# Warm columns copied on chip, one loop for the keys, and early loads of x2 in a two-layer image kernel

## Chip, cores and metric

The kernel runs on one core of a Trainium2 chip. The metric is the device time in microseconds (us); lower is better. PE is the matmul engine, ACT, DVE and POOL are the scalar, vector and GpSimd engines, SP issues most DMAs.

## What is computed

The input x is [2, 64, 256, 256] in f32; the kernel sees it as 128 rows (batch times channel) of 65536 tokens. Four residual steps follow each other:

```python
x = x + shift_conv3x3(ln_c(x))                     # stage A; gives x1
t = t + recurrence(ln_t(t))                        # y_t = sigmoid(Wx_t + V y_{t-1}), Wx batch-normalized; gives x2
x = x + linear_attention(ln_c(x))                  # keys and values from every 4th row and column; gives x3
t = t + experts(ln_t(t))                           # top 8 tokens of each of 32 experts, two-layer FFN, scatter-add
# linear attention:
xs = x[:, :, 2::4, 2::4]                           # 4096 positions: the keys' stage
K = elu(k) + 1; V = v                              # kv = kv_w @ ln_c(xs) + kv_b
KV = sum_n K_n^T V_n (per head); Ksum = sum_n K_n
out = Q @ KV / (Q @ Ksum + eps); out = proj_w @ out + proj_b
```

## The kernel before

There are five stages, each a block of its own at whose end all engines meet.

**Stage A** (to 759 us) does the convolution and the projection W x and leaves x1 and the projected rows (`xl`) in DRAM.

**Region stage** (766 to 1081 us). The recurrence is cut into 8 regions of 8192 tokens, each region into 512 chunks of 16 tokens; one step advances all 512 chunks of a region at once. Since a chunk doesn't know the state at its start, it runs 12 warm steps over the last 12 inputs of the chunk in front (`WARM`), then its 16 own steps. A region lies in SBUF as `U[r % 4]`, [128, 16, 1 + 512]: column 0 holds the last chunk of the region in front, of which `load_warm` (L750) fetches the last 12 inputs from DRAM, in pieces of 4 bytes. A step is a product by V on PE (L814), an add of the input on DVE (L910) and a sigmoid on ACT (L836 and L827), for two groups of 256 chunks. Two regions are in work at a time: region r's 28 steps begin at slot 14 r. At step 15 of a region DVE keeps a state (L881) and compares the state reached by the warm steps with the true one (`check_states`, L890 and L894). POOL adds y to x1, one block of 2048 tokens in 5.5 us (L849), then picks the keys' positions out of it into `xsub` (L655). SP's list, per block k: store x2 of block k, load x1 of block k + 3, load a block of region r + 4; ahead of the first block of a region also `load_warm`. For the last region x1 is loaded over a free region buffer.

A **sequential fallback** (L935 to L1009) follows, which isn't taken in these runs.

**Keys' stage** (1081 to 1133 us). First a loop over 8 tiles of 512 keys (L1039, L1074, L1097): center on PE (L1043), square on ACT (L1079), mean of squares on PE (L1048), log and exp on ACT (L1084, L1088), scale on DVE (L1099). Then a loop over 16 pairs of 128-key groups (L1049, L1089, L1100): product with the key and value weights (L1056), bias on DVE (L1105), exp on ACT (L1093), max and min-add on DVE (L1111, L1113), and two matmuls for each group: the sum of K V (L1064) and the sum of K (L1066, one column of ones). At the end the masking by heads (L1117, L1118) and the product with the projection (L1069), copied at L1120.

**Attention stage** (1133 to about 1680 us): 32 blocks of x2 in a ring of 8 (`x2_ring`), loaded by `load` (L1234), four ahead of the first statistics. Squares (L1367 on ACT, L1439 on POOL), statistics (L1307, L1313), rstd to DRAM (L1240) and back as a broadcast (L1249), query (L1322, L1476), its map on ACT, POOL (L1444) and DVE, denominator, L1451 on POOL, attended (L1334), x3 (L1491), gates and top tokens. The **experts** close the kernel.

Of the kernel before, what the change touches and what calls it, by code (L numbers as in the profile page):

```python
# [7 lines left out]
F32 = mybir.dt.float32  # L8
I32 = mybir.dt.int32
U32 = mybir.dt.uint32  # L10
ALU = mybir.AluOpType
# [56 lines left out]
def build_program(nc, x, conv_k, ffn_w, ffn_v, gamma, beta, q_w, q_b, kv_w, kv_b, proj_w, proj_b,  # L68
# [4 lines left out]
    with stack:  # L73
# [568 lines left out]
        regions = ExitStack()  # L642
        stack.enter_context(regions)
        BUFS = 4
        U = [sb(f"region{j}", [P, CLEN, 1 + CHUNKS], F32, regions) for j in range(BUFS)]
# [4 lines left out]
        last_stored = sem("last_stored", keys)  # L650

# [8 lines left out]
        with ExitStack() as ph:  # L660
# [21 lines left out]
            dstep, dmm, zero_warm, last_x1_loaded = S("dstep"), S("dmm"), S("zero_warm"), S("last_x1_loaded")  # L682
# [50 lines left out]
            def wait_group(eng, r, j):  # L733

                b = r % BUFS
                warm_loads = r // BUFS + (1 if b else 0)
                eng.wait_ge(region_loaded[b][0], 16 * (GB * (r // BUFS + 1) + warm_loads))
                if j:
                    eng.wait_ge(region_loaded[b][j], 16 * GB * (r // BUFS + 1))
                elif r == 0:  # L740
                    eng.wait_ge(zero_warm, 1)

            @blk.sync
            def _(sp):
# [4 lines left out]

                def load_warm(r):  # L750
                    sp.dma_start(U[r % BUFS][:, CLEN - WARM:CLEN, 0:1],
                                 xl_d[r * RBLK - 1, :, :].rearrange("p (n c) -> p n c", n=CLEN)[:, CLEN - WARM:CLEN, BLOCK // CLEN - 1:BLOCK // CLEN],
                                 allow_slow_non_contiguous=True).then_inc(region_loaded[r % BUFS][0], 16)
# [20 lines left out]
                for k in range(LAST):  # L774
# [69 lines left out]
            def _(pool):  # L844
                pool.memset(U[0][:, :, 0:1], 0.0).then_inc(zero_warm, 1)
# [165 lines left out]

        with ExitStack() as ph:
            RING = 3
# [3 lines left out]
            t_kv = sb("t_kv", [P, RING, 2, 2 * P], F32, ph)  # L1017
            ek = sb("ek", [P, RING, 2, P], F32, ph)
            gm = sb("gm", [P, P], F32, ph)
            psa = [ph.enter_context(nc.psum_tensor(f"psa{j}", [P, TILE], F32)) for j in range(3)]  # L1020
            psb = ph.enter_context(nc.psum_tensor("psb", [P, TILE], F32))
            pkv = [ph.enter_context(nc.psum_tensor(f"pkv{j}", [P, 2, 2 * P], F32)) for j in range(2)]
            pg = ph.enter_context(nc.psum_tensor("pg", [P, P], F32))
            psum_k = ph.enter_context(nc.psum_tensor("psum_k", [P, 1], F32))
            pm = psb[:, 0:P]
            S = lambda n: sem(n, ph)
# [4 lines left out]
            NPAIR = NSUB // P // 2  # L1031

            @blk.sync
            def _(sp):
                sp.wait_ge(last_stored, 16 * RBLK)

            @blk.tensor
            def _(pe):
                for t in range(KT + 1):  # L1039
                    if t < KT:  # L1040
                        if t >= 3:
                            pe.wait_ge(kn, t - 2)
                        pe.matmul(psa[t % 3][:, :], center, xsub[:, t * TILE:(t + 1) * TILE], start=True, stop=True).then_inc(kc, 1)  # L1043
                    if t:
                        pe.wait_ge(ksq, t)
                        if t >= 2:
                            pe.wait_ge(kln, t - 1)
                        pe.matmul(psb[:, :], meanm, sqk[:, (t - 1) % 2, :], start=True, stop=True).then_inc(kv_, 1)  # L1048
                for c in range(NPAIR + RING - 1):  # L1049
                    if c < NPAIR:  # L1050
                        if c % (TILE // P // 2) == 0:
                            pe.wait_ge(kn, c // (TILE // P // 2) + 1)
                        if c >= 2:
                            pe.wait_ge(kvb_done, c - 1)
                        for i in range(2):
                            m = pe.matmul(pkv[c % 2][:, i, :], xsub[:, (2 * c + i) * P:(2 * c + i + 1) * P], kvT[:, :],  # L1056
                                          start=True, stop=True)
                        m.then_inc(kvp, 1)
                    d = c - (RING - 1)
                    if d >= 0:  # L1060
                        pe.wait_ge(kmap, d + 1)
                        for i in range(2):
                            first, last = d == 0 and i == 0, d == NPAIR - 1 and i == 1
                            pe.matmul(pg[:, :], t_kv[:, d % RING, i, P:2 * P], t_kv[:, d % RING, i, 0:P], start=first,  # L1064
                                      stop=last)
                            m = pe.matmul(psum_k[:, :], t_kv[:, d % RING, i, 0:P], ones[:, :], start=first, stop=last)  # L1066
                        m.then_inc(kvacc, 1)
# [821 lines left out]
```

## Time and profile before

| | us |
|---|---|
| median of 3 runs | 1936.65 (1932.2 to 1941.81) |
| profiled execution | 1939.52 |
| its span | 1937.7 |
| PE, DVE, ACT, POOL busy | 1562.9, 1440.2, 1237.0, 1451.2 |

Times in the profile count from the span's start. A row of the timeline gives start, length, engine, line of the code, operation, output and input tensors, and in square brackets the idle time in front of it and what ended it. "PEld" is the loading of weights, "SPq" the issuing of DMAs. An f32 matmul shows as two instructions.

### The profile page before, as it was taken

How to read it: one execution, taken by the hardware profiler on the slowest of the kernel's cores; microseconds unless marked ns; L12 is line 12 of the kernel's file. 1: busy time of each engine (PE TensorE's matmuls, PEld its weight loads, DVE VectorE, ACT ScalarE, POOL GpSimd, SP SyncE). 2: the span in 40 equal slices, each digit the busy share in tenths (PEclk: the TensorE clock that was granted, in tenths of full speed). 3: DMA queues.
4: the chain of work that ended last, by engine and by line, in shares of the span. 5: the costliest groups of instructions: out<-in, count | busy, mean ns of one | idle time of the engine just before them, and what ended most of it. 6: DMA issues, size and time to landing. Idle time of an engine off the chain costs nothing. (4 is left out here: it accounts for less than half of the span.)

```text
span 1937.7 us, 24495 instructions
## 1 busy us (share of the span) xinstructions
PE 1562.9 (81%) x5690; PEld 655.8 (34%) x5690; DVE 1440.2 (74%) x2310; ACT 1237.0 (64%) x2171; POOL 1451.2 (75%) x1070
## 2 busy tenths in 40 slices
PE   4899999999999983788786678999999999816100
PEld 1333333333333330356553343333333333205100
DVE  1689999999999984588887537999999999951000
ACT  2777777777777751588775448888888888620000
POOL 2999999999999990067777109999999999901670
PEclk8999999999999996799988779999999999955555
DMA  4578878888888655999996246888888888570111
GB/s 152 160 230 251 254 233 254 250 255 242 248 257 238 205 167 173 293 300 354 365 386 256 87 152 200 285 284 280 277 280 288 285 289 244 189 192 14 2 2 1
DMA packets 125343, 429.87 MB, mean 222 GB/s; under 512 B 57585, under 2 KB 62609, under 8 KB 80145
## 3 DMA queue, kind: packets, MB, share of 16 engines
q1 hardware_dynamic: 103520, 423.82, 69.2%
q10 hardware_dynamic: 18736, 4.29, 1.5%
q8 instruction: 50, 0.82, 0.2%
q0 software_dynamic: 2944, 0.18, 0.1%
q14 instruction: 93, 0.75, 0.1%
HBM read 257.93 MB, written 170.01 MB: 221 GB/s over the span
## 5 line engine op out<-in xcount | busy, mean ns | idle before, releaser
L454 ACT ACTIVATE tap_products<-xn,kk 128x512 f32<-128x512 f32 x384 | 275.2, 718 | 165.2 <-POOL x_and_products L485 159.8
L485 POOL TENSOR_TENSOR x_and_products<-tap_products,x_and_products 128x512 f32<-128x512 f32 x256 | 326.7, 1276 | 41.7 <-POOL x_and_products L485 3.5
L385 PE MATMUL pst<-xn,taps 128*128 128x512 f32 x768 | 351.8, 593 | 0.0
L1444 POOL TENSOR_SCALAR exp_q<-exp_q 128x512 f32<-128x512 f32 x128 | 189.3, 1479 | 81.9 <-ACT exp_q L1395 81.9
L910 DVE SCALAR_TENSOR_TENSOR pss<-region,bn,pss 128x256 f32<-128x256 f32 x432 | 196.5, 489 | 68.6 <-PE pss L814 66.4
L849 POOL TENSOR_TENSOR x_block<-x_block,region 128x2048 f32<-128x2048 f32 x28 | 155.2, 5542 | 116.2 <-ACT region L836 86.5
L543 DVE SCALAR_TENSOR_TENSOR pst<-xn,kk,pst 128x512 f32<-128x512 f32 x256 | 192.5, 752 | 61.7 <-PE pst L385 61.5
L385 PEld LDWEIGHTS pst<-xn,taps 128*128 128x128 f32 x768 | 145.5, 190 | 186.2 <-issue 186.0
L1439 POOL TENSOR_TENSOR sq_norm<-x_ring 128x512 f32<-128x512 f32 x128 | 188.4, 1472 | 5.7 <-DVE x_ring L1491 1.7
L485 POOL TENSOR_TENSOR x_and_products<-tap_products,x_ring 128x512 f32<-128x512 f32 x128 | 164.2, 1283 | 19.6 <-ACT tap_products L454 19.6
L425 ACT ACTIVATE sq<-x_ring 128x512 f32<-128x512 f32 x256 | 157.7, 622 | 16.1 <-POOL x_ring L492 10.1
L492 POOL TENSOR_TENSOR x_ring<-acc,x_and_products 128x512 f32<-128x512 f32 x128 | 163.4, 1277 | 0.6 <-DVE acc L543 0.6
L1451 POOL TENSOR_TENSOR q_z<-q_map,z_inv 128x512 f32<-128x512 f32 x128 | 163.7, 1279 | 0.0
L814 PE MATMUL pss<-region,vT 128*128 128x256 f32 x480 | 136.3, 410 | 19.5 <-ACT region L836 19.5
L568 DVE TENSOR_TENSOR wx<-psw,rstd_wide 128x512 f32<-128x512 f32 x128 | 137.7, 1076 | 17.7 <-DMA rstd_wide<-rstd_scratch 7.0
L1328 PE MATMUL ps_denominator<-q_map,dT 128*128 128x512 f32 x256 | 138.6, 623 | 9.7 <-DVE q_map L1485 8.4
L814 PE MATMUL pss<-warm_state,vT 128*128 128x256 f32 x352 | 109.7, 436 | 44.4 <-ACT warm_state L836 26.4
L1322 PE MATMUL ps_query<-x_ring,qcT 128*128 128x512 f32 x256 | 140.1, 631 | 5.0 <-DVE query L1476 5.0
L394 PE MATMUL psc<-x_ring,cst 128*128 128x512 f32 x256 | 139.6, 628 | 4.5 <-DVE xn L520 4.5
L400 PE MATMUL psw<-x_ring,wcT 128*128 128x512 f32 x256 | 132.9, 603 | 11.7 <-DVE wx L568 11.7
L836 ACT ACTIVATE region<-pss,bn 128x256 f32<-128x256 f32 x256 | 117.0, 474 | 29.5 <-DVE pss L910 28.4
L1401 ACT ACTIVATE ln_d<-ps_denominator,cols 128x512 f32<-128x512 f32 x128 | 86.8, 678 | 73.0 <-PE ps_denominator L1328 72.7
(243 smaller groups left out, 2981.0 us busy)
## 6 DMA issues: line engine op xcount, KB each, us to landing
rstd_wide<-rstd_scratch SPq DMA_DIRECT2D x128, 512.0 KB, 7.3
x_ring<-in_x SPq DMA_DIRECT2D x32, 1024.0 KB, 5.3
x_scratch<-x_ring SPq DMA_DIRECT2D x32, 1024.0 KB, 4.3
xl_scratch<-wx SPq DMA_DIRECT2D x32, 1024.0 KB, 8.7
region<-xl_scratch SPq DMA_DIRECT2D x32, 1024.0 KB, 11.4
x_ring<-x_scratch SPq DMA_DIRECT2D x32, 1024.0 KB, 5.2
rstd_of_channels<-rstd_scratch SPq DMA_DIRECT2D x64, 512.0 KB, 7.7
out<-x_ring SPq DMA_DIRECT2D x32, 1024.0 KB, 6.7
```

The source lines that it names most:

```text
L385: m = pe.matmul(wide(pst[g % 2]), taps[:, n * P:(n + 1) * P], tap_rows(g, t), start=(n == 0), stop=(n == len(PE_TAPS) - 1))
L425: act.activation(sq[l][:, g % TPB, :], x_tile(g), ACT.Square).then_inc(squared[l], 1)
L454: act.activation(prod[:, n, :, :], tap_rows(g, t), ACT.Copy, scale=kk[:, t:t + 1]).then_inc(products, 1)
L485: pool.tensor_tensor(xr[:, g % XR, :], prod[:, n, :, :].rearrange("p r w -> p (r w)"), xr[:, g % XR, :] if n else x_tile(g), ALU.add).then ...
L492: pool.tensor_tensor(x_tile(g), acc[:, g % 2, :, :].rearrange("p r w -> p (r w)"), xr[:, g % XR, :], ALU.add).then_inc(x1_ready, 1)
L543: dve.scalar_tensor_tensor(out=out, in0=tap_rows(g, t), scalar=kk[:, t:t + 1], in1=wide(pst[g % 2]), op0=ALU.mult, op1=ALU.add).then_inc(a ...
L814: pe.matmul(ps_at(r, j), vT[:, :], before, start=True, stop=True).then_inc(carried, 1)
L849: pool.tensor_tensor(in_chunks(x1_x2), in_chunks(x1_x2), y, ALU.add).then_inc(added, 1)
L910: dve.scalar_tensor_tensor(out=ps_at(r, j), in0=u, scalar=gain_w, in1=ps_at(r, j), op0=ALU.mult, op1=ALU.add).then_inc(summed, 1)
L1439: pool.tensor_tensor(sq[1][:, g % SQSLOTS[1], :], x_tile(g), x_tile(g), ALU.mult).then_inc(squared[1], 1)
L1444: pool.tensor_scalar(e, e, 1.0, None, ALU.min).then_inc(clipped, 1)
L1451: pool.tensor_tensor(qz[:, g % 2, :], qm[:, g % QSLOTS, :], zr[:, g % 2, :], ALU.mult).then_inc(qz_ready, 1)
```

## The change

Three parts. (1) The warm inputs of region r + 1 are no longer loaded: ACT copies them from the last column of region r, in front of region r's first sigmoid of the second group, before the states overwrite them. (2) The two loops of the keys' stage become one of 24 steps; the sum of K rides as a 129th column of the sum of K V, whose operands swap sides, so that a transpose and a copy are added at the end. (3) The ring of x2 is allocated in front of the keys' stage, and SP issues the loads of its first six blocks at the start of that stage. `xsub` lives on, and two buffers of the attention stage lie in it.

```diff
@@ region stage
             def wait_group(eng, r, j):
                 b = r % BUFS
-                warm_loads = r // BUFS + (1 if b else 0)
-                eng.wait_ge(region_loaded[b][0], 16 * (GB * (r // BUFS + 1) + warm_loads))
+                eng.wait_ge(region_loaded[b][0], 16 * GB * (r // BUFS + 1))
                 if j:
                     eng.wait_ge(region_loaded[b][j], 16 * GB * (r // BUFS + 1))
                 elif r == 0:
-                    eng.wait_ge(zero_warm, 1)
+                    eng.wait_ge(warm_ready, 1)
+                else:
+                    eng.wait_ge(warm_ready, r + 1)
...
-                    if r:
-                        load_warm(r)
...
                             sp.wait_ge(checked, r + 1)
-                            load_warm(r + BUFS)
...
+                def copy_warm(r):
+                    if r >= BUFS:
+                        act.wait_ge(checked, r - BUFS + 1)
+                    act.activation(U[r % BUFS][:, CLEN - WARM:CLEN, 0:1],
+                                   U[(r - 1) % BUFS][:, CLEN - WARM:CLEN, CHUNKS:CHUNKS + 1], ACT.Copy).then_inc(warm_ready, 1)
...
                             if s == 0:
                                 wait_group(act, r, j)
+                                if j == GROUPS - 1 and r + 1 < REGIONS:
+                                    copy_warm(r + 1)
@@ keys' stage
+        SLOTS, SEMS, AHEAD = 8, 3, 6
+        def load_x2(sp, k):
+            if k >= SEMS:
+                sp.wait_ge(x2_loaded[k % SEMS], 16 * (k // SEMS))
+            sp.dma_start(X[:, k % SLOTS, :], x2_d[k, :, :]).then_inc(x2_loaded[k % SEMS], 16)
...
-            RING = 3
+            RING = 4
+            V1 = P + 1
...
+            PAIRS = TILE // P // 2
+            SECOND, PRODUCT, SUM = 1, 6, 8
+            STEPS_K = NPAIR + SUM
...
             @blk.sync
             def _(sp):
+                for k in range(AHEAD):
+                    load_x2(sp, k)
                 sp.wait_ge(last_stored, 16 * RBLK)
...
+                def add_pair(p):
+                    pe.wait_ge(kmap, p + 1)
+                    pe.wait_ge(kst, 1)
+                    for i in range(2):
+                        m = pe.matmul(pg[:, :], t_kv[:, p % RING, i, 0:P], t_kv[:, p % RING, i, P:P + V1],
+                                      start=(p == 0 and i == 0), stop=(p == NPAIR - 1 and i == 1))
+                    m.then_inc(kvacc, 1)
+
+                for c in range(STEPS_K):
+                    if (t := tile_in(c, 0)) is not None:
+                        center_keys(t)
+                    if (p := pair_in(c, PRODUCT)) is not None:
+                        product(p)
+                    if (t := tile_in(c, SECOND)) is not None:
+                        second_moment(t)
+                    if (p := pair_in(c, SUM)) is not None:
+                        add_pair(p)
+                pe.wait_ge(kst, 2)
+                pe.transpose(pgt, gm[:, :], ident).then_inc(kmm, 1)
+                pe.wait_ge(kst, 4)
+                pe.matmul(pm, gv[:, :], pT[:, :], start=True, stop=True).then_inc(kmm, 1)
...
+                for c in range(STEPS_K):                       # ACT
+                    if (t := tile_in(c, 0)) is not None:
+                        square(t)
+                    if (t := tile_in(c, SECOND)) is not None:
+                        rsqrt(t)
+                    if (p := pair_in(c, PRODUCT)) is not None:
+                        exp_keys(p)
...
+                for c in range(STEPS_K):                       # DVE
+                    if (p := pair_in(c, PRODUCT)) is not None:
+                        add_bias(p)
+                    if (p := pair_in(c, PRODUCT + 1)) is not None:
+                        map_keys(p)
+                    if (t := tile_in(c, SECOND + 1)) is not None:
+                        norm(t)
...
@@ attention stage
-                    if (k := block_at(t, LOAD)) is not None:
+                    if (k := block_at(t, LOAD)) is not None and k >= AHEAD:
                         load(k)
```

`tile_in(c, lag)` is the tile whose work of that lag falls into step c (every second step), `pair_in` the pair.

## Rows read from the trace of the kernel before

**Rows 1.** Windows: stretch, length; busy of PE, PEld, DVE, ACT, POOL; clock, DMA, GB/s.
```profile
1081.00:1086.00 5.00, 4.35 (x6) 1.93 (x7) 0.00 (x0) 2.45 (x3) 0.00 (x0) 0.53 0.66 267
1103.00:1131.00 28.00, 26.56 (x182) 24.27 (x183) 20.87 (x48) 6.66 (x16) 0.00 (x0) 1.00 0.01 1
1200.00:1600.00 400.00, 400.00 (x1527) 130.01 (x1527) 376.46 (x564) 351.65 (x616) 396.69 (x287) 1.00 0.88 282
```

**Rows 2.** Timeline of the region stage, POOL's adds and DVE's comparison L890.
```profile
865.52 5.54 POOL L849 TENSOR_TENSOR x_block<-x_block,region 128x2048 f32<-128x2048 f32 x1 [5.96 <-ACT region L836]
869.84 1.77 DVE L890 TENSOR_TENSOR reached<-reached,region 128x512 f32<-128x512 f32 x1
...
895.77 5.54 POOL L849 TENSOR_TENSOR x_block<-x_block,region 128x2048 f32<-128x2048 f32 x1 [5.17 <-ACT region L836]
...
929.17 5.53 POOL L849 TENSOR_TENSOR x_block<-x_block,region 128x2048 f32<-128x2048 f32 x1 [2.98 <-ACT region L836]
930.35 4.91 DVE L890 TENSOR_TENSOR reached<-reached,region 128x512 f32<-128x512 f32 x1
...
963.82 5.53 POOL L849 TENSOR_TENSOR x_block<-x_block,region 128x2048 f32<-128x2048 f32 x1 [2.86 <-ACT warm_state L827]
964.56 5.33 DVE L890 TENSOR_TENSOR stats<-stats,region 128x512 f32<-128x512 f32 x1
...
996.69 5.53 POOL L849 TENSOR_TENSOR x_block<-x_block,region 128x2048 f32<-128x2048 f32 x1
998.93 3.83 DVE L890 TENSOR_TENSOR reached<-reached,region 128x512 f32<-128x512 f32 x1
```

**Rows 3.** Page, DMA issues of load_warm; windows without and with one such load.
```profile
region<-xl_scratch SPq DMA_DIRECT2D x7, 6.0 KB, 9.0
852.00:875.00 23.00, 19.28 (x82) 12.60 (x81) 20.71 (x44) 19.07 (x45) 16.85 (x7) 0.98 1.01 380
875.00:890.00 15.00, 15.00 (x63) 10.44 (x62) 13.72 (x31) 13.51 (x31) 14.13 (x5) 0.92 1.03 347
```

**Rows 4.** Groups by line, keys' stage: busy us, mean ns, idle before.
```profile
L1105 DVE TENSOR_TENSOR t_kv<-pkv,kvb 128x512 f32<-128x512 f32 x16 | 11.0, 691 | 5.6 <-PE pkv L1056 5.6
L1113 DVE SCALAR_TENSOR_TENSOR t_kv<-ek,t_kv 128x256 f32<-128x256 f32 x16 | 6.8, 425 | 0.6
L1093 ACT ACTIVATE ek<-t_kv 128x256 f32<-128x256 f32 x16 | 6.7, 416 | 20.3 <-DVE t_kv L1105 20.3
...
L1084 ACT ACTIVATE lnk<-psb,cols 128x512 f32<-128x512 f32 x8 | 5.5, 687 | 2.3 <-PE psb L1048 1.9
L1088 ACT ACTIVATE rsk<-lnk 128x512 f32<-128x512 f32 x8 | 5.0, 630 | 0.3
L1079 ACT ACTIVATE sqk<-psa 128x512 f32<-128x512 f32 x8 | 4.7, 590 | 1.9 <-PE psa L1043 1.9
L1111 DVE TENSOR_SCALAR t_kv<-t_kv 128x256 f32<-128x256 f32 x16 | 4.5, 284 | 0.0
```

**Rows 5.** Timeline of the keys' stage, PE and its weight loads.
```profile
1081.65 3.75 PE L1043 MATMUL psa<-xsub,cst 128*128 128x512 f32 x4 [16.00 <-PEq L935]
...
1086.30 1.02 PE L1043 MATMUL psa<-xsub,cst 128*128 128x512 f32 x2
...
1107.53 0.73 PEld L1056 LDWEIGHTS pkv<-kvT,xsub 128*128 128x128 f32 x4
...
1108.36 0.34 PEld L1064 LDWEIGHTS pg<-t_kv 128*128 128x128 f32 x2
```

**Rows 6.** Timeline, end of the keys' stage and start of the attention stage.
```profile
1131.42 0.29 DVE L1117 TENSOR_TENSOR gm<-pg,cst 128x128 f32<-128x128 f32 x1 [1.37 <-PE psum_k L1066]
...
1132.86 1.28 ACT L1360 ACT_TABLE_LOAD   x1 [3.69 <-PEq L1012]
...
1137.67 2.19 ACT L1367 ACTIVATE sq_norm<-x_ring 128x512 f32<-128x512 f32 x4 [3.52 <-DMA x_ring<-x_scratch]
...
1154.51 1.29 DVE L1476 TENSOR_TENSOR query<-ps_query,rstd_of_channels 128x512 f32<-128x512 f32 x2 [6.87 <-DMA rstd_of_channels<-rstd_scratch]
```

More of the change, by code:

```diff
@@ L641, in build_program @@
         gain_w = bn[:, 6:7]
[L642 to L645, printed above, removed]
         keys = ExitStack()
@@ L650, in build_program @@
         last_stored = sem("last_stored", keys)
+        regions = ExitStack()
+        stack.enter_context(regions)
+        BUFS = 4
+        U = [sb(f"region{j}", [P, CLEN, 1 + CHUNKS], F32, regions) for j in range(BUFS)]
         def take_keys(pool, block, src_rows):
@@ L1031, in build_program, with tile_in, pair_in @@
             NPAIR = NSUB // P // 2
+            PAIRS = TILE // P // 2
+            SECOND, PRODUCT, SUM = 1, 6, 8
+            STEPS_K = NPAIR + SUM
+            def tile_in(c, lag):
+                t, rest = divmod(c - lag, PAIRS)
+                return t if rest == 0 and 0 <= t < KT else None
+            def pair_in(c, lag):
+                p = c - lag
+                return p if 0 <= p < NPAIR else None
             @blk.sync
             def _(sp):
+                for k in range(AHEAD):
+                    load_x2(sp, k)
                 sp.wait_ge(last_stored, 16 * RBLK)
@@ L1049, in _ @@
[L1049 to L1067, printed above, removed]
@@ new lines, in product @@
+                def product(p):
+                    pe.wait_ge(kn, p // PAIRS + 1)
+                    if p >= 2:
+                        pe.wait_ge(kvb_done, p - 1)
+                    for i in range(2):
+                        m = pe.matmul(pkv[p % 2][:, i, :], xsub[:, (2 * p + i) * P:(2 * p + i + 1) * P], kvT[:, :],
+                                      start=True, stop=True)
+                    m.then_inc(kvp, 1)
+                def add_pair(p):
+                    pe.wait_ge(kmap, p + 1)
+                    pe.wait_ge(kst, 1)
+                    for i in range(2):
+                        m = pe.matmul(pg[:, :], t_kv[:, p % RING, i, 0:P], t_kv[:, p % RING, i, P:P + V1],
+                                      start=(p == 0 and i == 0), stop=(p == NPAIR - 1 and i == 1))
+                    m.then_inc(kvacc, 1)
@@ L1089, in _, with square @@
-                for c in range(NPAIR):
-                    act.wait_ge(kvb_done, c + 1)
-                    if c >= RING:
-                        act.wait_ge(kmap, c - RING + 1)
-                    act.activation(ek[:, c % RING, :, :], t_kv[:, c % RING, :, 0:P], ACT.Exp).then_inc(kexp, 1)
+                def square(t):
+                    act.wait_ge(kc, t + 1)
+                    if t >= 2:
+                        act.wait_ge(kv_, t - 1)
+                    act.activation(sqk[:, t % 2, :], psa[t % 3][:, :], ACT.Square).then_inc(ksq, 1)
@@ L1095, in _ @@
+                for c in range(STEPS_K):
[5 more added lines that the diff above has]
+                        exp_keys(p)
             @blk.vector
             def _(dve):
-                for t in range(KT):
+                dve.memset(t_kv[:, :, :, 2 * P:2 * P + 1], 1.0).then_inc(kst, 1)
@@ L1164, in build_program @@
             S = lambda n: sem(n, ph)
-            SEMS = 3
-            x2_loaded = [S(f"x2_loaded{r}") for r in range(SEMS)]
             x3_stored = [S(f"x3_stored{r}") for r in range(SEMS)]
```

121 lines of the change are left out of this document (56 added, 65 removed).

## Prediction

> **What bounds the kernel now.** I read the windows first, stage by stage, because a share over the whole span mixes five stages. The long last main loop (channel attention, from 1132.86 us) is bound by POOL: 396.69 us busy of 400 [rows 1]. Whatever lets that loop begin earlier moves the end by as much, and whatever makes one of its other engines faster moves nothing. The keys' stage before it (1081.65 to 1132.86 us, 51.2 us) has two halves one after the other: the norm, in which PE, ACT and DVE wait for each other, and the products, in which 16 pairs take 28 us [rows 1, 5], so 1.75 us a pair, with weight loads following each other without a gap. The region stage (766 to 1081 us) is a chain PE, DVE, ACT; the timeline of DVE and POOL shows one odd thing in it.
>
> **Region stage: where it stalls.** Once in a region DVE compares states at L890. Here it took 1.77 us where POOL's running add of 5.54 us had begun 4.3 us before it, but 4.91, 5.33 and 3.83 us where that add had just begun [rows 2]. Each time DVE ends about 0.5 us after POOL does: 929.17 + 5.53 = 934.70, against 930.35 + 4.91 = 935.26. So the stall is set by the lag between the moment POOL's block could begin and the moment it does. In the undisturbed regions the first block of a region follows the one before by 30.25 us (865.52, 895.77 [rows 2]), so that of region 3 could have begun at 926.0; it began at 929.17, a lag of 3.2 us. L890 begins 4.35 us after that release; by the same 4.35 the releases of regions 4 and 5 are 960.2 and 994.6, their lags 3.6 and 2.1, and the regions between last 34.2 and 34.4 us instead of 30.25: a us of lag costs 1.15 to 1.25. POOL was free there, and what it adds (x1) is loaded by a queue that is full: DMA share 1.01, 380 GB/s [rows 3]. The Trainium skill, page SBUF — State Buffer, section Who interferes with whom, says that GpSimd and a VectorE instruction with two SBUF inputs hold a shared port for a whole instruction and the other blocks; these rows agree.
>
> **Part 1, warm columns.** Seven DMAs of 6 KB go from SP's queue [rows 3]; each has 1536 pieces of 4 bytes (128 partitions x 12 steps). Price of one: the stretch of 15 us with one of them moves 347 GB/s against 380 without [rows 3], so 15 x (1 - 347/380) = 1.3 us of a full queue; the two other such stretches that I looked at gave the like, and I take 1.25. The first three lie in the initial loads, before anything waits for them, and count as nothing. The later ones are issued ahead of the x1 loads of regions 3 and 4: three before block 12 (3.75 us), four before blocks 16 to 20 (5.0 us). Block 12 could then start at 929.17 - 3.75 = 925.4, but is released at 926.0: lag 0, gain 34.2 - 30.25 = 4.0. Block 16 then is released at 956.25 and starts at 963.82 - 5.0 = 958.8: lag 2.5 instead of 3.6, gain 1.2. Block 20: 996.69 - 5.0 = 991.7 against a release at 956.25 + 30.25 + 2.9 = 989.4: lag 2.3 instead of 2.1, loss 0.3. Sum 4.9, less the copies on ACT: seven instructions that the trace doesn't show. The nearest row is an ACT instruction of 256 columns, 0.416 us [rows 4]; 12 columns cost no more, so at most 2.9 us for all, at least nothing. What is queued behind a copy on ACT is the first sigmoid of the second group, and five of the seven come just ahead of a comparison whose end POOL fixes, so they vanish in it. The other two I take at 0.2 each. The waits that the copy adds are on states checked two regions ago and on loads that the next instruction wants anyway. **Region stage: -4.5**, bounds -10 (all lags gone: 4.0 + 4.1 + 2.4 less the copies) and +4 (the copies in full, and blocks landing so that one comparison more meets an add that has just begun).
>
> On small pieces the Trainium skill has a rule against this price: DMA: Bandwidth & Descriptors, section Why small descriptors are slow, gives some 3 cycles of overhead a packet. By that a warm load would be an estimated 96 x 4 cycles an engine, as much as 1.5 pieces of 8 KB, 0.5 us instead of 1.25, and the region stage would give some 2 us. The two windows decide for 1.25.
>
> **Part 2, the keys' loop.** Per tile of 512 columns there are one centering, one second moment and two pairs. PE: a pair's product is four instructions of 256 columns, with weight loads from 1107.53 to 1108.36 [rows 5], 0.83 us, 0.21 each. With 512 columns the two instructions of a centering or a second moment hold PE for twice that each, 0.85 us together (they show as 1.02 with the latency at their end). A pair's sums have the rest of 1.75, 0.92, for eight instructions. The change has four of these (the column of ones rides as the 129th), so 0.46. Per tile 2 x 0.85 + 2 x (0.83 + 0.46) = 4.3 us. DVE per tile: 0.69 (the norm, as long as the bias add) + 2 x (0.691 + 0.284 + 0.425) = 3.49; ACT: 0.590 + 0.687 + 0.630 + 2 x 0.416 = 2.74 [rows 4]. So PE is the bound where the loop is full, and the lag of the steps leaves each product at least 2.1 us of other PE work before its sum, against 1.7 us that a bias, a map and their hops need.
> Start: six steps carry no product. ACT does the square, then waits for the second moment, then log and exp, then the next square: 0.59 + 1.02 + 0.69 + 0.63 and hops = 3.0 us a tile, the first 4.1 (PE at its low clock in 1081 to 1086, granted 0.53 [rows 1]). With the first product allowed after the third second moment: 1081.65 + 4.1 + 3.0 + 3.0 = 1091.7.
> Full part: five tiles at 4.3 less the two sums not yet due, 5 x 4.3 - 0.92 = 20.6: to 1112.3.
> Drain: six pairs without norm, where the round product, bias, map, sum binds: DVE's 1.40 with gaps, 1.5 each, 9.0: to 1121.3, and the last pair's bias, the map before it, its own map and its sum (0.69 + 0.71 + 0.71 + 0.46 and hops) 2.8: 1124.1, where the old stage has its masking at 1131.42 [rows 6].
> Tail: the old one takes 1.44 us from there to the next stage (1132.86); the transpose and its copy add one more trip PE and DVE, 0.35 + 0.49 + 0.29 = 1.1. Next stage at 1126.6. **Keys: -6.3.** Bounds: if every tile of the full part costs PE and DVE waits as the old norm did (some 20% more, 4 us) -2; if start and drain overlap better, -9. Six x2 loads run meanwhile; DMA is idle in that stretch (0.01 [rows 1] in 1103 to 1131), so 6 MB at 380 GB/s, 17 us, fit into 45. SP holds nothing else then. Their cost is taken as nothing; if they weren't hidden, part 3 would be smaller.
>
> **Part 3, start of the attention.** Now ACT's first square waits for the first x2 block: 1137.67, where the table load begins at 1132.86 and takes 1.28 [rows 6], so it could be at 1134.1: -3.5. PE's sums of x then come early too, and the chain square, second moment, variance, rstd, DRAM, broadcast, first query at 1154.51 [rows 6] moves with it. PE comes out of a busy loop instead of 5 us of waiting, and the broadcast of 1 MB has no x2 load right behind it. Between 0 and 2 us more for both; I take 0.5. **-4.0**, bounds -3.5 and -5.5. Behind it POOL runs without a gap, so the shift reaches the end. The buffers that moved into xsub and the earlier ring change no order: nothing.
>
> **Sum.** -4.5 - 6.3 - 4.0 = -14.8. The profiled execution, 1939.52 us, of which 1937.7 are the span, would be 1924.7. It lies 2.9 above the median of the three runs, 1936.65; that median would be 1921.9.
>
> **Rivals.** (a) *The region stage gives nothing and the loop runs worse than its PE sum.* POOL's blocks reach the comparisons by chance, and a shift by 1 to 5 us can turn a lag of 0 (as in regions 1 and 2) into one of 3. For it: three of eight comparisons now vary by up to 3.6 us. Against: the blocks of regions 1 and 2 in the rows are released by ACT, not by a load. Region 0, keys -4, attention -3.5: -7.5, 1929.2. (b) *Slower: PE's clock.* In 1081 to 1086 the granted clock was 0.53, the low level (1.2 GHz), after 16 us without work, and 1.00 (2.4 GHz) in 1103 to 1131 [rows 1]. In the new start PE has 1.7 us of work in 3.0. Were the low level kept through the loop, a tile would be 8.6 us: 12 + 5 x 8.6 - 1.8 + 6 x 2.6 + 6 = 75 us instead of 51, +24, and with the two other terms +15.5: 1952. It outweighs all gain from 3.4 tiles at the low level (14.8 / 4.3). Against: the norm part of before, where PE also waits for ACT, went at the high level (two instructions of 512 columns in 1.02 us at 1086.30 [rows 5]). The Trainium skill, TensorE: Matmul & The Clock Gate, section What's actually happening, says that the low level is the default and activity releases it; on a loop with PE as its bound it speaks for the full level. (c) *The x2 loads are hidden anyway or don't run early.* If they waited for the stage's end part 3 would be 0: -10.8, 1925.9. SP's list has them first, so little speaks for it.
>
> **Chances.** Forecast with its own spread 0.64, (a) 0.22, (c) 0.06, (b) 0.05, the rest (a cause that no row shows) 0.03. About 0.5%, 9.7 us, is what a measurement of this kernel can tell from no change (its three runs spread by as much). Of the forecast and (c), some 0.68 end beyond it; (a) is within it, as is what is left of the forecast: 0.26; slower 0.06. The range takes (a) in with some noise, above, and the bounds of the region stage and the keys together, below: 1911 to 1932.
>
> **What would show it.** L890 at 1.8 us also in region 3, the second stretch of DMA at 375 GB/s or more; the warm copy at some 0.2 us on ACT. Keys' stage 45 us, PE idle only in its first 10 and last 12 us, clock 1.00 from its first 5 us on. Attention: no wait for x2, first query 17 to 18 us after the stage begins (21.65 now); POOL without gaps from then. Wrong if L890 stays at 4 to 5 us, if a step of the loop shows PE waiting for the map, or if the clock falls in the loop.

## Result, and the profile after

| | before | after |
|---|---|---|
| median, 15 runs each | 1936.65 us (1931.28 to 1941.81) | 1925.02 us (1920.68 to 1929.09) |
| ratio, 95% interval | 1 | 0.9945 (0.9933 to 0.9956) |
| profiled execution, its span | 1939.52, 1937.7 | 1924.74, 1922.9 |
| PE, DVE, ACT, POOL busy | 1562.9, 1440.2, 1237.0, 1451.2 | 1556.5, 1435.2, 1238.3, 1450.8 |

The change saves 11.6 us; 14.8 had been forecast. The busy time of POOL is the same within 0.4 us; what moved is when the long loop begins. (Two of the six runs of experiment 7 fell into a slower state, at a lower granted clock, and are left out of its time.) So the trace is best read as a ledger of stages: each stage's length from the first row of one to the first row of the next. The columns are the region stage (first DMA issued to the first centering of the keys), the keys' stage, the attention stage up to its first query, and from there to POOL's last work in it.

| us | region | keys | to first query | then |
|---|---|---|---|---|
| before | 315.2 | 51.2 | 21.65 | 543.3 |
| before, profiled again | 315.1 | 51.3 | 21.67 | 543.3 |
| after | 309.8 | 45.8 | 18.1 | 543.6 |
| after, profiled again | 310.6 | 49.4 | 18.3 | 543.3 |
| after, a third time | 311.2 | 47.4 | 17.7 | 542.9 |
| mean difference | **-4.6** | **-3.7** | **-3.6** | 0.0 |
| forecast | -4.5 | -6.3 | -4.0 | 0 |

The three sum to -11.9, and the medians differ by 11.6. The two first profiles alone differ by 14.8, the forecast to the tenth, but by luck: in the one of after stage A came out 2.3 us shorter and the experts 1.5 us longer, and the keys' stage was the shortest of three.

Three profiles are few. The kernel of experiment 3 has the region stage of after as it is, that of experiment 7 too; theirs took 312.2 and 307.4 us. Over the five profiles the stage takes 307.4 to 312.2 us, 310.2 in the mean, which is 4.9 under before. The keys' stage of after stands unchanged in the kernels of experiments 3, 8, 9 and 10, where it took 46.3, 46.0, 47.4 and 46.3 us; over seven profiles the mean is 46.9, 4.3 under before.

**Region stage.** The timeline of after answers [rows 2]: L893 is the comparison, L852 POOL's add, L820 the new copy on ACT.

```profile
924.00 5.54 POOL L852 TENSOR_TENSOR x_block<-x_block,region 128x2048 f32<-128x2048 f32 x1 [2.59 <-ACT region L839]
928.32 1.77 DVE L893 TENSOR_TENSOR reached<-reached,region 128x512 f32<-128x512 f32 x1
...
957.70 5.54 POOL L852 TENSOR_TENSOR x_block<-x_block,region 128x2048 f32<-128x2048 f32 x1 [2.34 <-DMA x_block<-x_scratch]
957.71 0.21 ACT L820 ACTIVATE region<-region 128x12 f32<-128x12 f32 x1
958.57 5.22 DVE L893 TENSOR_TENSOR stats<-stats,region 128x512 f32<-128x512 f32 x1
...
993.09 3.22 DVE L893 TENSOR_TENSOR reached<-reached,region 128x512 f32<-128x512 f32 x1
```

The add of block 12 is released by ACT, 4.3 us ahead of the comparison, which takes 1.77 us where it took 4.91. (In [rows 2] the profile puts that add down to ACT as well; in the second profile of before it waits 2.85 us for its load.) Block 16 still waits for its load, and the comparison beside it still takes 5.22 us. The windows show the queue (columns as in [rows 1]; the first is a stretch of [rows 3], the second the stretch of another warm load, in which before moved 343 GB/s, the third lies in the long loop).

```profile
875.00:890.00 15.00, 15.00 (x68) 10.21 (x67) 14.84 (x34) 14.39 (x34) 12.53 (x6) 0.99 1.02 377
911.00:926.00 15.00, 14.40 (x64) 9.24 (x62) 14.19 (x32) 14.16 (x32) 10.17 (x5) 1.00 1.01 368
1180.00:1600.00 420.00, 419.17 (x1597) 136.15 (x1596) 394.78 (x592) 369.72 (x647) 416.61 (x301) 1.00 0.88 283
```

The first stretch moves 377 GB/s, where a warm load had left 347 [rows 3]. In the last line POOL is busy for 416.61 of 420 us, and PE for 419.17. The prediction named POOL as the bound of this loop; PE's row is as full, here and in [rows 1], and no run tells the two apart. What the account needs, that the loop passes on whatever comes earlier, is shown by the last column of the ledger, which doesn't change.

**Keys' stage.** PE's rows at the start of the new loop, centering (L1076), second moment (L1082) and first product (L1089):

```profile
1074.05 2.05 PE L1076 MATMUL psa<-xsub,cst 128*128 128x512 f32 x2 [16.00 <-PEq L938]
1076.78 2.08 PE L1082 MATMUL psb<-sqk,cst 128*128 128x512 f32 x2 [0.69 <-ACT sqk L1123]
...
1081.06 1.12 PE L1082 MATMUL psb<-sqk,cst 128*128 128x512 f32 x2 [0.69 <-ACT sqk L1123]
...
1084.11 1.12 PE L1082 MATMUL psb<-sqk,cst 128*128 128x512 f32 x2 [1.07 <-ACT sqk L1123]
...
1085.93 1.89 PE L1089 MATMUL pkv<-kvT,xsub 128*128 128x256 f32 x8
...
1117.65 0.29 DVE L1182 TENSOR_TENSOR gm<-pg,cst 128x128 f32<-128x128 f32 x1 [0.81 <-PE pg L1097]
```

A second moment is two instructions of 512 columns: 2.08 us for the pair of them shows the low clock (1.2 GHz), 1.12 the high one (2.4 GHz). Tiles are 4.28 us apart, then 3.05. From the first product to the masking (L1182) it is 31.7 us.

**Attention stage.** The rows that answer to [rows 6]:

```profile
1119.82 1.28 ACT L1411 ACT_TABLE_LOAD   x1 [3.84 <-PEq L1031]
1121.11 2.71 ACT L1418 ACTIVATE sq_norm<-x_ring 128x512 f32<-128x512 f32 x5
...
1137.96 1.29 DVE L1527 TENSOR_TENSOR query<-ps_query,rstd_of_channels 128x512 f32<-128x512 f32 x2 [6.02 <-DMA rstd_of_channels<-rstd_scratch]
```

The square starts when the table is loaded, with no wait for x2 in front (3.52 us before). The first query comes 18.14 us into the stage, against 21.65.

### The profile page after: what moved, and what is told of

It reads as the page before. It is cut to its first block and busy times, and to the rows that moved or that the text cites. A ratio compares the mean times of both kernels' runs of the same rounds, so it can differ in the third digit from the quotient of the medians.

```text
span 1922.9 us, 24399 instructions
## 1 busy us (share of the span) xinstructions
PE 1556.5 (81%) x5627; PEld 648.4 (34%) x5627; DVE 1435.2 (75%) x2312; ACT 1238.3 (64%) x2178; POOL 1450.8 (75%) x1070
## 5 line engine op out<-in xcount | busy, mean ns | idle before, releaser
L852 POOL TENSOR_TENSOR x_block<-x_block,region 128x2048 f32<-128x2048 f32 x28 | 155.3, 5545 | 110.8 <-ACT region L839 88.5
L425 ACT ACTIVATE sq<-x_ring 128x512 f32<-128x512 f32 x256 | 157.6, 622 | 16.7 <-POOL x_ring L492 10.1
L807 PE MATMUL pss<-region,vT 128*128 128x256 f32 x480 | 137.5, 411 | 18.4 <-ACT region L839 18.2
L400 PE MATMUL psw<-x_ring,wcT 128*128 128x512 f32 x256 | 132.9, 603 | 11.6 <-DVE wx L568 11.6
L839 ACT ACTIVATE region<-pss,bn 128x256 f32<-128x256 f32 x256 | 116.6, 474 | 29.4 <-DVE pss L913 28.7
```

The source lines that it names most:

```text
L425: act.activation(sq[l][:, g % TPB, :], x_tile(g), ACT.Square).then_inc(squared[l], 1)
L807: pe.matmul(ps_at(r, j), vT[:, :], before, start=True, stop=True).then_inc(carried, 1)
L852: pool.tensor_tensor(in_chunks(x1_x2), in_chunks(x1_x2), y, ALU.add).then_inc(added, 1)
```

## Experiments: which part gives what

**1. Warm copies alone.** The kernel before, with part 1 of the change only: `copy_warm` on ACT in place of `load_warm`.

```diff
-                    if r:
-                        load_warm(r)
...
                             if s == 0:
                                 wait_group(act, r, j)
+                                if j == GROUPS - 1 and r + 1 < REGIONS:
+                                    copy_warm(r + 1)
```

> The kernel before with part 1 alone (warm columns copied by ACT). Theory (three terms that add up; the warm loads' share of a full DMA queue sets the lag of POOL's adds): the region stage, from its first DMA issue to the first centering of the keys, goes from 315.2 us to 309 to 311, L890 in region 3 at 1.8 us instead of 4.9; the total falls by 4 to 6 us. Rival (chance alignment of POOL's adds and DVE's comparisons, the warm loads not the cause): the stage lies anywhere between 309 and 318, total within 2 us of before.

Measured: 1934.25 us, ratio 0.9987 (0.997 to 1.0003) to before in the same session, as in all that follow; region stage 310.9 us, -4.3, the other stages within 0.1 us.

```profile
911.00:926.00 15.00, 14.39 (x65) 9.34 (x64) 14.82 (x34) 14.92 (x35) 10.76 (x4) 1.00 1.01 375
...
926.56 5.54 POOL L854 TENSOR_TENSOR x_block<-x_block,region 128x2048 f32<-128x2048 f32 x1 [2.25 <-DMA x_block<-x_scratch]
929.38 3.27 DVE L895 TENSOR_TENSOR reached<-reached,region 128x512 f32<-128x512 f32 x1
```

The stretch moves 375 GB/s where before moved 343, so a warm load costs 15 x (1 - 343/375) = 1.3 us of a full queue; the other stretch gives 1.2. The stage gains what the forecast had for it, though not by the same comparison each time: block 12 is held by its load here, and the comparison takes 3.27 us, where 1.8 had been expected. In the three profiles of after that comparison took 1.77, 4.58 and 3.16. The gain doesn't sit in one lag. One profile couldn't exclude the rival, chance alignment; that all six profiles whose kernel has the copies and no other edit in this stage have it at 307.4 to 312.2 us, against 315.1 twice, does speak for the copies. For the total 4 to 6 us had been expected; it gains 2.5 by the ratio, and the interval takes in no change: the runs bear out the 4.3 us in the stage, not in the time.

**2. Each warm load twice.** The kernel before, with an addition: a second load of the same 6 KB into spare memory.

```diff
 def load_warm(r):
+    sp.dma_start(spare[:, r - 1, :, 0:1], xl_d[...]).then_inc(spare_loaded, 16)
     sp.dma_start(U[r % BUFS][:, CLEN - WARM:CLEN, 0:1], xl_d[...]).then_inc(region_loaded[r % BUFS][0], 16)
```

> The kernel before with each warm load issued twice (the second into a spare tile that nothing reads, on a semaphore that is waited for at the end of the stage). Theory: the price doubles: each extra load takes 1.25 us of the full DMA queue, blocks 12 and 16 start 3 to 5 us later, region stage 317 to 321 us, total 2 to 6 us over before; the DMA rate in a stretch of 15 us around two such loads falls to 310 to 325 GB/s. Rival (packet overhead of some 0.5 us a load): at most 2 us in all, rate 335 or more.

Measured: 1939.08 us, ratio 1.0011 (0.9998 to 1.0024); region stage 317.5, +2.4. The stage is where it was expected; the total isn't clear of no change, and 2 to 6 us had been expected.

```profile
932.64 0.68 DVE L896 TENSOR_TENSOR reached<-reached,region 128x512 f32<-128x512 f32 x1
934.09 5.55 POOL L855 TENSOR_TENSOR x_block<-x_block,region 128x2048 f32<-128x2048 f32 x1 [4.63 <-DMA x_block<-x_scratch]
...
875.00:890.00 15.00, 15.00 (x65) 10.40 (x64) 14.11 (x32) 13.62 (x32) 12.18 (x5) 0.94 0.95 276
...
ACT warm_state L833 <- DMA region<-xl_scratch: 5.6, 1, 5.6
```

The queue falls to 276 GB/s in this stretch and to 296 in 911 to 926, further than the 310 to 325 expected of a doubled price. POOL's add (block 8 here) waits 4.63 us for its load. The comparison now ends before the add begins, and takes 0.68 us: that is its own duration with POOL idle. So the stall isn't in the comparison's work. A later POOL even frees it: the next two comparisons take 0.68 us as well. That would explain why twice the loads cost the stage only 2.4 us, though ACT now waits once for a region's load (5.6 us, last line; its columns are total, count, longest). The step of the forecast "a us of lag costs 1.15 to 1.25" holds only up to the point where the add starts behind the comparison.

**3. The early loads of x2 away.** The kernel after, with the six loads at their old place.

```diff
-        SLOTS, SEMS, AHEAD = 8, 3, 6
+        SLOTS, SEMS, AHEAD = 8, 3, 0
```

> The changed kernel without the early loads (parts 1 and 2 only; all x2 loads in the attention stage as before). Theory: keys' stage 45.5 to 46 us as in the changed kernel, first query 21.5 us after the attention stage begins instead of 18.1, total 3.5 us over the changed kernel. Rival (the early loads cost the keys' loop or are hidden anyway): keys' stage shorter than 45.5 and the total within 1 us of the changed kernel.

Measured: 1929.95 us, ratio 0.9966 (0.9953 to 0.9979), 3.2 us over after in that session (1926.79, below); keys' stage 46.3, to the first query 21.3.

```profile
1124.52 1.28 ACT L1411 ACT_TABLE_LOAD   x1 [4.15 <-PEq L1031]
...
1129.30 2.19 ACT L1418 ACTIVATE sq_norm<-x_ring 128x512 f32<-128x512 f32 x4 [3.50 <-DMA x_ring<-x_scratch]
```

The wait for x2 is back, 3.50 us, and with it 3.2 us of the stage. Part 3 is worth that, and the loads cost the keys' stage nothing that can be seen: 46.3 without them, 45.8 to 49.4 with them, and from the first product to the masking 31.7 us either way. Rival (c) falls.

**4, 5, 6. The same kernels again.** The keys' stage in the first profile of after was 45.8 us; is that its length?

> The changed kernel itself. Theory: stages as in its first profile, region 309, keys 45.8, start of the attention 18.1 us, total 10 to 15 us under before. Rival (its first profile was a lucky one): a region stage of 312 us or more.

> The kernel before, once more, for its stages. Theory: region stage 315 +- 1 us, keys 51.2, first query 21.6 us after the stage begins; what differs between executions is the clock in the first microseconds of a stage and the experts' part. Rival: the region stage varies by 3 us or more with how POOL's adds fall against DVE's comparisons, so that the gain read there from one pair of profiles says little.

> The changed kernel, a third profile. Theory: region 309 to 311 us; keys' stage 45.8 or, if PE's clock rises late, up to 49.4. Rival: it rises as early as in the first profile nearly always, keys 45.8 to 46.3.

Measured: after 1926.79 us, ratio 0.9941 (0.9919 to 0.9963), and 1929.23 in a single run; before 1941.14 in a single run. Before repeats its stages to 0.1 us; after's keys' stage is 49.4 and 47.4, where the first had 45.8, so the first profile was a lucky one in this stage. PE in the former, and the windows over it:

```profile
1079.65 2.07 PE L1082 MATMUL psb<-sqk,cst 128*128 128x512 f32 x2 [0.69 <-ACT sqk L1123]
...
1084.12 2.07 PE L1082 MATMUL psb<-sqk,cst 128*128 128x512 f32 x2 [0.69 <-ACT sqk L1123]
...
1088.58 2.07 PE L1082 MATMUL psb<-sqk,cst 128*128 128x512 f32 x2 [0.69 <-ACT sqk L1123]
...
1092.16 2.17 PE L1089 MATMUL pkv<-kvT,xsub 128*128 128x256 f32 x8
...
1082.00:1086.00 4.00, 3.31 (x5) 0.85 (x4) 0.69 (x1) 1.68 (x3) 0.00 (x0) 0.50 1.01 424
1086.00:1090.00 4.00, 3.31 (x5) 1.16 (x4) 0.69 (x1) 1.91 (x3) 0.00 (x0) 0.50 1.01 418
1094.00:1098.00 4.00, 4.00 (x18) 2.84 (x17) 3.04 (x8) 2.86 (x6) 0.00 (x0) 1.00 0.35 145
```

The granted clock is 0.50, the low level (1.2 GHz), until 1092.7, 15.8 us after the loop began, with PE busy for 3.31 us of 4; in the first profile it rises 6.0 us in, and the pair at 1081.06 was fast. A tile then takes 4.46 us instead of 3.05, and the first product comes 15.2 us after the first centering instead of 11.9 (third profile: the clock rises 11.3 us in, the product comes at 13.5). From the first product to the masking all three take 31.7 to 32.0. So nearly the whole spread of the stage lies in its start, and goes with the clock there.

## Experiments: what can still be had

**7. Two edits at the starts.** The kernel after, with the second moment of a tile two steps later, so that two centerings stand ahead of the first wait and ACT isn't waited for in each tile; and without the loading of the ACT table at the start of the attention stage (the keys' stage has left the same table in place).

```diff
-            SECOND, PRODUCT, SUM = 1, 6, 8
+            SECOND, PRODUCT, SUM = 3, 6, 8
...
-                act.preload_act_table_set("natural_log_exp_and_others")
```

> The changed kernel with the second moment two steps later in the keys' loop (so that the next tile's centering and square run ahead of it) and without the table load at the head of the attention stage, whose table is the one of the keys' stage. Theory: start of the loop 2.1 us a tile instead of 3.05, keys' stage 2 to 3 us shorter, and less hanging on when PE's clock rises; attention's first square 1.3 us earlier, first query 16.9 us after the stage's begin instead of 18.2; total -3 to -4. Rival (PE's total work bounds the stage, the start is hidden in it): keys' stage unchanged at 45.8.

Measured: 1920.4 us (four runs), ratio 0.9911 (0.9883 to 0.9939) to before; keys' stage 42.4, to the first query 16.7.

```profile
1076.31 1.20 PE L1082 MATMUL psb<-sqk,cst 128*128 128x512 f32 x2
...
1078.38 1.10 PE L1082 MATMUL psb<-sqk,cst 128*128 128x512 f32 x2
...
1080.63 1.89 PE L1089 MATMUL pkv<-kvT,xsub 128*128 128x256 f32 x8
...
1115.20 2.71 ACT L1417 ACTIVATE sq_norm<-x_ring 128x512 f32<-128x512 f32 x5 [3.97 <-PEq L1031]
```

Tiles of the start are 2.07 us apart, PE has no gap of 0.69 us for the square, and the first second moment, 3.6 us after the first centering, already goes nearly at the high clock. The first product comes 7.9 us after the start. From there to the masking it is 32.3 us, 0.3 to 0.6 more than in after: only the start was gained. The square of the attention stage begins with the stage, 1.3 us earlier. Not all of the total is the edit's: the region stage is that of after, but came out at 307.4 us, 3.1 under the mean of three. The stages, not the total, say what the edits are worth: 4.5 to 5.1 us in the keys' stage, by the mean it is held against, and 1.3 in the next.

**8. The last region's adds all on DVE.** After the last comparison DVE and POOL add two blocks each. The kernel after, so changed that DVE adds all four.

```diff
-            POOL_LAST = (1, 3)
+            POOL_LAST = ()
```

> The changed kernel with all four last adds of y on DVE instead of two on POOL. Theory (DVE's and POOL's adds take turns at the shared input, so the end is their sum: 5.7 us each on POOL, some 3.7 each on DVE): from the last sigmoid to the end of the last add 15 to 16 us instead of 18.9, total -3. Rival (they run side by side and DVE's 12 us are its own two adds of 6): 24 us, total +5.

Measured: 1921.53 us, ratio 0.9912 (0.9889 to 0.9935). First two lines of after, then two of this kernel.

```profile
1051.31 5.39 DVE L893 TENSOR_TENSOR reached<-reached,region 128x512 f32<-128x512 f32 x1 [0.54 <-ACT region L839]
1057.54 11.99 DVE L925 TENSOR_TENSOR region<-region 128x2048 f32<-128x2048 f32 x2
```

```profile
1053.76 0.69 DVE L893 TENSOR_TENSOR reached<-reached,region 128x512 f32<-128x512 f32 x1 [0.54 <-ACT region L839]
1055.29 15.08 DVE L925 TENSOR_TENSOR region<-region 128x2048 f32<-128x2048 f32 x4
```

With POOL idle the four adds take DVE 15.08 us, 3.8 each. Of the two in after the first took 8.24 us, begun beside POOL's second add and ended 3.7 after it, and the second 3.83. So DVE didn't work more slowly beside POOL; it waited for it, in the comparison and in its first add. The adds take DVE's time after POOL's, and two engines finish this work later than one: from the comparison's start to the end of the adds it is 18.2 us with both, 16.6 with DVE alone. That is 1.6 gained, where 3 had been expected. The median is 3.5 under that of after; what is above the 1.6 isn't explained by the edit.

**9. The comparison's subtraction on POOL.** The kernel after; POOL subtracts ahead of the region's first add, DVE only reduces, and SP waits for the subtraction.

```diff
+                def subtract_states(r):
+                    pool.wait_ge(y_ready, y_done(r))
...
+                    pool.tensor_tensor(d, d, U[r % BUFS][:, CLEN - 1, 0:CHUNKS], ALU.subtract).then_inc(subtracted, 1)
...
                         if s == HALF + 1 and r:
                             keep_state(r)
+                        if s == HALF + 3 and r:
                             check_states(r - 1)
```

> The changed kernel with the subtraction of the state comparison on POOL, ahead of the region's first add, and DVE's reduction two steps later; SP waits for the subtraction where it waited for the comparison. Theory (the stall is DVE waiting for POOL's running add through its second SBUF input, and is paid on the chain): no stall of 2.7 us and more at the comparison, regions follow each other in 27.5 to 28 us instead of 30.2 to 34, region stage 290 to 298 us instead of 309, unless the DMA queue (8.4 us a block, 33.6 us a region) takes over, in which case it is 298 to 305 with waits for the region's load. Rival (the stall is DVE's own, from reading one column of a strided tile): POOL's subtraction is as long and something else is late; region stage 306 us or more.

Measured: 1925.57 us, ratio 0.994 (0.992 to 0.996); region stage 304.6, 5.9 less than the mean of after. The profiled execution took 1922.22 us. The ratio is that of after (0.9945), so the gain shows in the stage of one profile and not in the time.

```profile
951.26 5.53 POOL L853 TENSOR_TENSOR x_block<-x_block,region 128x2048 f32<-128x2048 f32 x1 [2.29 <-ACT warm_state L840]
957.22 1.26 POOL L862 TENSOR_TENSOR stats<-stats,region 128x512 f32<-128x512 f32 x1
958.51 0.69 DVE L903 TENSOR_REDUCE dmax<-stats 128x1 f32<-128x512 f32 x1 [5.13 <-POOL stats L862]
```

The stall is now an idle time in front of DVE's reduction, 5.13 us: POOL's add of an older block stands ahead of the subtraction. Part of the wait only changed its name. The subtraction itself takes POOL 1.26 us, and ACT waits once for a region's load (6.6 us): of what had been expected, the case in which the DMA queue takes over (298 to 305 us) is the one that fits.

**10. The reduction later.** Kernel 9 with the reduction six slots later.

```diff
-                        if s == HALF + 3 and r:
+                        if s == HALF + 9 and r:
```

> As sub_pool, but DVE's reduction eight steps after the old comparison instead of two. Theory (in sub_pool DVE waited for POOL's subtraction, which stood behind POOL's adds in their queue, so the wait had only changed its name): with the reduction late enough no wait of more than 1 us is left at it, the regions follow each other in 27.5 to 28.5 us until the DMA queue holds POOL's blocks, region stage 295 to 301 us (sub_pool 304.6, the changed kernel 309.8). Rival (the chain is held by the DMA queue already): 303 to 305 as in sub_pool.

Measured: 1920.39 us, ratio 0.992 (0.9901 to 0.9939); region stage 304.9, the same as in 9. The theory had 295 to 301; the rival, 303 to 305, came true.

```profile
916.84 0.59 ACT L831 ACTIVATE warm_state<-region,bn 128x256 f32<-128x256 f32 x1
943.72 0.59 ACT L831 ACTIVATE warm_state<-region,bn 128x256 f32<-128x256 f32 x1
...
979.59 0.60 ACT L831 ACTIVATE warm_state<-region,bn 128x256 f32<-128x256 f32 x1 [7.33 <-DMA region<-xl_scratch]
...
1047.42 0.69 DVE L903 TENSOR_REDUCE dmax<-reached 128x1 f32<-128x512 f32 x1 [16.60 <-POOL reached L862]
```

While nothing stalls, regions are 26.9 us apart (916.84 to 943.72) instead of 30.25. But then ACT waits 7.33 us for a region's load, and at the end DVE waits 16.60 for POOL, which itself had waited 25.6 us in all for x1. Each comparison's stall is gone, and waits for loads have taken its place. That the queue now bounds the stage is how I read these rows; no run took traffic off it to test that.

**11, 12. Together.** Kernel 11 is 7, 8 and 9 in one; kernel 12 is 7, 8 and 10.

> The changed kernel with the three edits of sub_pool, last_dve and starts together. Theory: their gains are in stages one after the other and add up: 12 to 20 us under the changed kernel, 1905 to 1913. Rival (the region stage is held by the DMA queue once the stalls are gone): 6 to 9 us under it.

> The changed kernel with sub_pool_late, last_dve and starts together. Theory: stages add up: region 292 to 298 us, keys 42.5 to 43, first query after 16.7; total 1905 to 1911. Rival (what the region stage gains is lost to the last adds or to x1 loads that come later): 1913 to 1916 as all_four.

Measured: 1914.96 us, ratio 0.9881 (0.9861 to 0.9902), and 1914.99, ratio 0.9885 (0.9864 to 0.9907). Stages of 11: region 303.0, keys 42.9, to the first query 16.7; of 12: 302.7, 42.2, 16.5. Both are some 10 us (0.5%) faster than after and 22 to 24 faster than before in their sessions. The later reduction adds nothing to 11, as experiment 10 had it. Stage by stage the parts do add up: 310.5 - 5.9 (experiment 9) - 1.6 (experiment 8) is the 303.0 of the region stage. Neither kernel came to the 1913 and 1911 us at the upper end of what was expected, because the region stage had been expected at less than experiments 9 and 10 gave. For kernel 12 the rival theory, 1913 to 1916, is the one that held.

## Why the prediction was right, and where it was off

**Time, range and direction** held: 1925.0 for 1921.9, inside 1911 to 1932. The miss of 3.1 us is nearly all in one term.

**Region stage, -4.5 forecast, -4.3 alone and -4.6 in the mean.** The price of a warm load (1.25 us) was measured as 1.2 to 1.3. (By their packets alone it is less: 96 on each of 16 engines, 9.1 ns each in the trace of before, 0.87 us.) By the rule of the Trainium skill, page DMA: Bandwidth & Descriptors, section Why small descriptors are slow, the estimate had been 0.5 us; the trace doesn't agree. In detail the sum was less good than its total. Comparisons of regions 3 and 4 are now 928.32 and 958.57, 30.25 us apart, where they were 34.2: the 4.0 of the forecast, but in this profile only. In the second that interval is 33.75 us, in the third 31.7. The next interval is 34.5 (34.4 before): the 1.2 that was to be gained there isn't. The one after is 31.6 (33.45 before, from 998.93 to L890's next at 1032.38): 1.8 that I hadn't counted. So that the total of this term came out at -4.3 to -4.6 is in part luck. The copies on ACT cost 0.21 us each, inside the bound.

One thing in it the prediction had no term for. It took 30.25 us as the undisturbed distance of two regions. The second profile of after has shorter ones; the windows go from comparison to comparison (columns as in [rows 1]).

```profile
840.10:868.76 28.66, 25.03 (x109) 16.42 (x109) 26.53 (x59) 24.86 (x58) 24.07 (x9) 1.00 0.94 337
868.76:897.44 28.68, 25.04 (x109) 16.45 (x110) 26.54 (x60) 24.83 (x58) 24.16 (x9) 1.00 1.01 377
897.44:927.73 30.29, 26.66 (x109) 17.91 (x109) 26.71 (x59) 25.00 (x58) 21.36 (x9) 0.94 1.01 365
```

The comparison takes 1.8 us in all three. Where PE's mean granted clock is 1.00 a region takes 28.7 us, where it is 0.94 it takes 30.3, and in before it is 0.94 in each of the regions that the prediction calls undisturbed. PE waits for ACT around each comparison (2.41 us in front of 843.36 in before) and then runs its next products at the low level. So 1.6 us of a region's length goes with the clock after the stall, and with it about half of what the regions gain in experiment 10 (clock 1.00, 26.9 us).

**Keys' stage, -6.3 forecast, -3.7 measured: the term that was mis-sized.** The working had the first product 10.05 us after the start (4.1 + 3.0 + 3.0), then 32.4 us to the masking and 2.5 to the next stage. Measured: 11.9, 15.2 and 13.5 (mean 13.5), 31.7 to 32.0, and 2.2. The PE sum of the full part and the drain was right within 0.7 us; the start was 3.5 us too short. Two things were missing from its sum. First, the code puts the fourth tile's centering in front of the first product; that is 0.86 us at the high level (1085.07 to 1085.93) and 1.71 at the low one (1090.45 to 1092.16 in the second profile). Second, the low clock was taken to end with the first tile ("4.1", then 3.0 and 3.0), from the rows of the old loop [rows 5], where four instructions of centering stood in a row (3.75 us) and the next were fast 4.6 us after the start. The new loop begins with two, then waits 0.69 us for ACT in each tile, and stayed at 0.50 for 6.0 to 15.8 us: its first three tiles took 4.6, 3.4 and 3.05 us in the first profile, 4.6, 4.5 and 4.5 in the second. Rival (b) named this mechanism. Its 12 us for a start at the low level were near what the second profile has for these three tiles (13.5); what it had wrong is that the low level would last through the full part of the loop, which it did in no profile. In the start a tile at the low level cost 1.4 us more (4.46 - 3.05).

Experiment 7 shows the other side: with two centerings in a row at the start the clock rose after 3.9 us, and in the two kernels of experiments 11 and 12, which begin in the same way, after 5.1 and 3.0. In the four profiles of the old loop it rose after 3.9 to 5.4 us, in seven of the new one, started as in after, after 6.0 to 15.8. That goes with how a loop starts; why the same kernel needs 6 us once and 15.8 another time stays open. The Trainium skill, page TensorE: Matmul & The Clock Gate, section What's actually happening, has activity release the low level; the trace agrees.

**Attention, -4.0 forecast, -3.6 measured.** The sure part, the wait for x2 of 3.5 us, was right (3.2 in experiment 3). The extra 0.5 wasn't there: from the issue of the broadcast to the first query it took 7.4 us in both kernels (1130.54 to 1137.96 here), and the first second moment of the stage went at the low clock.

```profile
1123.35 1.94 PE L1364 MATMUL ps_second<-sq_norm,stat 128*32 128x512 f32 x8 [2.43 <-ACT sq_norm L1418]
...
1130.54 1.12 SPq L1300 DMA_DIRECT2D rstd_of_channels<-rstd_scratch  x2
```

**Rivals.** (a), nothing in the region stage and a poor loop, is refuted by experiment 1 in its first half. Its second half, -4 for the keys, is what was measured (-3.7, or -4.3 over seven profiles), though not for its reason: the full part of the loop went as PE's sum has it. (c) fell with experiment 3.

**Signs.** Named beforehand were L893 at 1.8 us in region 3 (true in one profile of three), 375 GB/s in the second stretch, 875 to 890 (377, 375 and 366), the copy at 0.2 us (0.21), the first query at 17 to 18 us (17.7 to 18.3), and the clock at 1.00 from the first 5 us of the keys' loop on, which was false (it rose 6.0, 15.8 and 11.3 us in) and was the larger part of the error.

## What to carry over

When an instruction's duration varies and its end keeps a fixed distance from another engine's, it is waiting, though the profile calls it busy; look for the lag between the two, and what sets it. A loop that begins after an idle stretch should be priced at the low clock for several of its iterations, or begin with matmuls that wait for nobody. And once a stall is gone, look at the full queue next to it: here moving the reduction later took the last stall away and gained nothing in the stage, because waits for loads stood behind it. Last, take a stage from several profiles before you call its gain by the tenth: this one's keys' stage varied by 3.6 us, and the first profile was the shortest.

## What the runs showed of the hardware

- A DVE subtraction of 128 x 512 with both inputs in SBUF took 0.68 us with POOL idle and 1.77 to 5.6 beside POOL's adds, ending 0.55 us after POOL's add in each of the eight comparisons of before and of after. DVE's add of 128 x 2048 took 3.8 us alone, and 8.24 when it was begun beside POOL's add, ending 3.7 after it. The profile counts such waiting as busy time.
- A load of 6 KB in 4-byte pieces cost a full queue 1.2 to 1.3 us (343 and 347 against 375 and 376 GB/s over 15 us); two in one stretch cost more than twice that (276 against 376). As an ACT copy the same data took 0.21 us.
- PE stayed at the low clock for 6.0, 15.8 and 11.3 us in three profiles of the same kernel, in a loop in which it waited 0.69 us in each tile; with four instructions in a row at the start it rose after 3.0 to 5.1 us in three others.
- In the recurrence, a region with a stretch at the low clock behind its comparison took 30.3 us, one without 28.7.
